# Last stage reordered into pairs of units, three banks for the up products and a ring of two for the rest; last states of the scan copied by ScalarE

## The reference, cut to what matters

```python
def _L1_attn_ref(...):          # x: 4096 tokens x 256, D_INNER = 512, N_STATE = 16
    ...
    def step(h, t):
        dt_t, B_t, C_t, u_t = t
        dA = jnp.exp(dt_t[:, :, None] * A)
        h = dA * h + (dt_t * u_t)[:, :, None] * B_t[:, None, :]
        return (h, jnp.einsum('bdn,bn->bd', h, C_t))
...
def _L1_ffn_ref(x, Wm, bm, expert_emb, W1, b1, W2, b2, Wo, bo):
    H, E, K = (8, 16, 2)         # heads of 32 features, experts, experts taken
    h = x @ Wm + bm
    t = h.reshape(bs * L_ * H, HD)
    w = jax.nn.softmax(t @ expert_emb, axis=-1)
    topw, topi = jax.lax.top_k(w, K)
    hmid = jax.nn.gelu(jnp.einsum('td,edi->tei', t, W1) + b1, approximate=False)
    eo = jnp.einsum('tei,eio->teo', hmid, W2) + b2
    sel = jnp.take_along_axis(eo, topi[:, :, None], axis=1)
    return (sel * topw[:, :, None]).sum(axis=1).reshape(bs, L_, d) @ Wo + bo
```

## Time and profile before

| | us |
|---|---|
| median of 3 runs | 3472.85 (3467.34 to 3473.31) |
| the profiled execution, its own time | 3465.27 |
| its span, first to last instruction | 3463.2 |
| first layer, up to about | 1665 |
| `layer1_scan`, about | 1665 to 2668 |
| `layer1_experts`: load and first routing | 2668 to 2722 |
| `layer1_experts`: 8 chunks | 2722 to 3441 |
| last projection, norm and store | 3441 to 3463 |

### The profile page before, as it was taken

One profiled execution on the slowest core, in us unless ns is written; L12 is line 12 of the kernel. 1 busy time (PEld: TensorE's weight loads), 2 busy tenths in 40 slices (PEclk: granted clock), 3 DMA queues, 4 the chain that ended last, 5 costly groups with the idle time before them and its releaser, 6 DMA issues. The chain is left out here.

```text
span 3463.2 us, 39510 instructions
## 1 busy us (share of the span) xinstructions
PE 3088.8 (89%) x11504; PEld 1701.8 (49%) x11504; DVE 2662.4 (77%) x3783; ACT 2282.6 (66%) x3239; POOL 2355.2 (68%) x1680
## 2 busy tenths in 40 slices
PE   3589999999999999998889999999976799999998
PEld 1156676666666667775334443443422333333332
DVE  5989898888988897554799999999996444544443
ACT  2457666666667666664666567666643488888887
POOL 3578888888888887773587888788783144444443
PEclk7689999999999999999899999999998799999999
DMA  2034444444444444553122222222221122222222
GB/s 94 13 97 128 122 128 126 127 121 119 131 123 121 124 120 130 146 148 87 61 68 70 71 69 69 71 70 68 71 70 55 53 99 99 105 105 104 103 101 86
DMA packets 199618, 335.38 MB, mean 97 GB/s; under 512 B 21379, under 2 KB 57380, under 8 KB 199020
## 3 DMA queue, kind: packets, MB, share of 16 engines
q1 hardware_dynamic: 199404, 332.86, 32.1%
HBM read 325.69 MB, written 7.09 MB: 96 GB/s over the span
## 5 line engine op out<-in xcount | busy, mean ns | idle before, releaser
L1435 POOL TENSOR_TENSOR c_hc<-c_h,c_c_rep 128x1024 f32<-128x1024 f32 x256 | 602.8, 2358 | 208.2 <-DVE c_h L1486 150.6
L1916 POOL TENSOR_TENSOR d_acc<-d_acc,d_prod 128x512 f32<-128x512 f32 x240 | 318.6, 1328 | 473.6 <-DVE d_prod L1984 473.2
L1486 DVE TENSOR_TENSOR_SCAN c_h<-c_decay,c_carry,c_v_ps 128x512 f32<-128x512 f32 x512 | 628.5, 1263 | 0.0
L1876 ACT ACTIVATE d_hmid<-d_up,d_b 128x1024 f32<-128x1024 f32 x512 | 539.7, 1112 | 78.4 <-PE d_up L1777 78.0
L1336 ACT ACTIVATE c_decay<-c_dt,c_a_cols 128x512 f32<-128x512 f32 x512 | 356.6, 718 | 337.0 <-DVE c_h L1486 319.9
L1186 PE MATMUL c_y_ps<-c_hc,ident 128*128 128x512 f32 x1024 | 507.1, 619 | 68.1 <-POOL c_hc L1435 56.1
L704 POOL TENSOR_TENSOR ab_inner_low<-ab_inner,ab_inner_high 128x512 fp32r<-128x512 f32 x264 | 341.1, 1292 | 239.5 <-ACT ab_inner_high L570 236.5
L559 ACT ACTIVATE ab_gate_ps<-ab_gate_ps,ab_raw_d 128x512 f32<-128x512 f32 x264 | 174.3, 660 | 445.7 <-PE ab_gate_ps L411 445.2
L1984 DVE SCALAR_TENSOR_TENSOR d_prod<-d_eo,d_b,d_w_rep 128x512 f32<-128x512 f32 x240 | 180.2, 751 | 314.9 <-PE d_eo L1787 172.8
L686 POOL TENSOR_TENSOR ab_hc<-ab_h,ab_c_rep 128x512 f32<-128x512 f32 x256 | 330.9, 1293 | 74.4 <-DVE ab_h L767 69.6
L1777 PE MATMUL d_up<-d_heads,d_w 128*128 128x512 f32 x1024 | 335.4, 434 | 16.6 <-ACT d_hmid L1876 9.4
(11 more groups left out here) (239 smaller groups left out, 6585.8 us busy)
## 6 DMA issues: line engine op xcount, KB each, us to landing
ab_raw_gu<-in_b_experts SPq DMA_DIRECT2D x264, 256.0 KB, 3.5
ab_w_rep<-ab_w_scratch SPq DMA_DIRECT2D x264, 256.0 KB, 3.7
c_c_rep<-c_c_scratch SPq DMA_DIRECT2D x256, 256.0 KB, 3.2
d_w_rep<-d_w_scratch SPq DMA_DIRECT2D x256, 256.0 KB
ab_raw_d<-in_b_experts SPq DMA_DIRECT2D x264, 129.0 KB, 2.1
ab_raw_x<-in_xT SPq DMA_DIRECT2D x32, 256.0 KB, 4.7
out<-xT SPq DMA_DIRECT2D x8, 512.0 KB, 3.4
xT<-in_xT SPq DMA_DIRECT2D x1, 3072.0 KB, 12.6
```

What stands on the lines that cost most here:

```text
L1435: nc.gpsimd.tensor_tensor(hc[:, q % HC], h[:, q % HR], c_rep[:, q % BC].unsqueeze(1).broadcast_to([P, PAIR, CH]), ALU.mult).then_inc(hc_re ...
L1486: nc.vector.tensor_tensor_scan(out=h[:, q % HR, m, :], data0=decay[:, i % DEC, :], data1=v_ps[m][:], initial=carry[:, i:i + 1], op0=ALU.mu ...
L1876: nc.scalar.activation(hmid[:, (2 * q + r) % HM], up_ps[r][:], ACT.Gelu, bias=b1[:, e:e + 1]).then_inc(gelu_ready, 1)
L1916: nc.gpsimd.tensor_tensor(acc[:, s, g, :], acc[:, s, g, :], prod[:, q % PR, :], ALU.add).then_inc(add_ready, 1)
```

## The change

**Scan.** `keep_last_states` moves from VectorE to ScalarE, as a copy of two columns per partition, behind the decays of unit `q`, for unit `q` - 4 (for q < 4 the last four units of the chunk before). The first scan of a unit now waits for that copy (`carry_ready`), as the copy must have read the slot of `h` that the scan overwrites.

**Experts, banks.** UP goes from 2 to 3 (six banks). The two banks left are a ring: all downs, the 13 items, the out projections, mean and variance take them in turn, in the order of the list `ring_uses`. Before a product, `take` waits for whoever reads the bank two uses before. HM goes from 4 to 8.

**Experts, order.** TensorE goes by pairs `u` of units: four `up` calls (eight products), then the two `down`s of the pair before, then items: halves at u = 0, 1; two heads each at u = 2..5; LOGITS at 6; TURN at 7; the variance of two chunks ago at 8 (before: of the last chunk, at q = 24); both out projections at 9, where the pair's last `up` comes behind them; mean at 10; BACK at 13. ScalarE and VectorE follow, two heads at a time.

```diff
@@ layer1_scan, scalar
+            def keep_last_states(c, q):
+                act.wait_ge(h_ready, c * NT + (q + 1) * PAIR + DEC)
+                nc.scalar.copy(carry[:, q * PAIR:(q + 1) * PAIR], h[:, q % HR, :, CH - 1]).then_inc(carry_ready, 1)
...
+                    if q >= HR:
+                        keep_last_states(c, q - HR)
+                    elif not first:
+                        keep_last_states(c - 1, NU - HR + q)
@@ layer1_scan, vector
-                    dve.wait_ge(carry_ready, c * NU + q + 1)
+                    dve.wait_ge(carry_ready, c * NU + q + 1 + NU - HR)
...
-            def keep_last_states(c, q):
-                dve.wait_ge(h_ready, c * NT + (q + 1) * PAIR + DEC)
-                nc.vector.reduce_max(carry[:, q * PAIR:(q + 1) * PAIR], h[:, q % HR, :, CH - 1:CH], axis=AX_X
-                                     ).then_inc(carry_ready, 1)
@@ layer1_experts
-    HM, UP, EO, PR, WR = 4, 2, 2, 4, 8
+    HM, UP, EO, PR, WR = 8, 3, 2, 4, 8
+    PAIRS = NU // 2
...
+    U_HALF, U_HEADS, U_LOGITS, U_TURN, U_VAR, U_OUT, U_MEAN, U_BACK = (0, 1), (2, 3, 4, 5), 6, 7, 8, 9, 10, 13
+    Q_SCALE, Q_EXP, Q_PICK, Q_SQUARE = 20, 17, 18, 23
+    def pair_uses(c, u):
+        if u > 0 or c > 0:
+            yield from (("down", c if u > 0 else c - 1, (2 * u - 2 + j) % NU) for j in range(2))
...
+        def bank(kind, c, i=0):
+            return ring[number[kind, c, i] % 2]
...
+            def take(kind, c, i=0):
+                at = number[kind, c, i]
+                if at >= 2:
+                    kind, c, i = ring_uses[at - 2]
+                    if kind == "down":
+                        pe.wait_ge(prod_ready, c * NU + i + 1 + EO)
+                    elif kind == "out":
+                        pe.wait_ge(norm.z_ready, c * 2 + i + 1 + norm.FREE)
+                    elif kind == "mean":
+                        pe.wait_ge(norm.zc_ready, c * 2 + 2)
+                    elif kind == "var":
+                        pe.wait_ge(norm.log_ready, c + 1)
...
@@ tensor, chunk
-                for q in range(NU):
+                for u in range(PAIRS):
                     for r in range(2):
-                        up(c, s, q, r)
-                    if q >= 1:
-                        down(c, q - 1)
-                    elif not first:
-                        down(c - 1, NU - 1)
...
+                        up(c, s, 2 * u, r)
+                    up(c, s, 2 * u + 1, 0)
+                    if u != U_OUT:
+                        up(c, s, 2 * u + 1, 1)
+                    for q in (2 * u - 2, 2 * u - 1):
+                        if q >= 0:
+                            down(c, q)
+                        elif not first:
+                            down(c - 1, NU + q)
                     if not last:
...
+                        if u in U_HEADS:
+                            product(c + 1, 1 - s, HEAD0 + 2 * (u - U_HEADS[0]))
+                            product(c + 1, 1 - s, HEAD0 + 2 * (u - U_HEADS[0]) + 1)
...
+                    if u == U_VAR and c >= 2:
+                        variance(c - 2)
+                    if u == U_OUT and not first:
+                        project_out(c - 1, 1 - s, 0)
+                        project_out(c - 1, 1 - s, 1)
+                    if u == U_MEAN and not first:
+                        mean(c - 1)
+                    if u == U_OUT:
+                        up(c, s, 2 * u + 1, 1)
```

More of the change, by code:

```diff
@@ L1605, in layer1_experts @@
     NADD = NU - GROUPS
-    HM, UP, EO, PR, WR = 4, 2, 2, 4, 8
+    HM, UP, EO, PR, WR = 8, 3, 2, 4, 8
+    PAIRS = NU // 2
     HEAD0, LOGITS, TURN, BACK = GROUPS, GROUPS + HEADS, GROUPS + HEADS + 1, GROUPS + HEADS + 2
     ITEMS = BACK + 1
-    Q_OUT, Q_MEAN, Q_CENTRE, Q_SQUARE, Q_VAR, Q_SCALE = 18, 20, 21, 23, 24, 20
-    Q_HALF, Q_HIGH, Q_LOW, Q_HEAD, Q_COPY = 0, 0, 1, 4, 5
-    Q_LOGITS, Q_KEEP_LOGITS, Q_TURN, Q_MAX, Q_EXP, Q_PICK, Q_BACK, Q_KEEP_WEIGHTS = 13, 13, 15, 16, 17, 18, 26, 26
+    U_HALF, U_HEADS, U_LOGITS, U_TURN, U_VAR, U_OUT, U_MEAN, U_BACK = (0, 1), (2, 3, 4, 5), 6, 7, 8, 9, 10, 13
[3 more added lines that the diff above has]
+            yield from (("down", c if u > 0 else c - 1, (2 * u - 2 + j) % NU) for j in range(2))
+        if c + 1 < NCH:
+            if u in U_HALF:
+                yield "item", c + 1, u - U_HALF[0]
+            if u in U_HEADS:
+                yield from (("item", c + 1, HEAD0 + 2 * (u - U_HEADS[0]) + j) for j in range(2))
+            for at, i in ((U_LOGITS, LOGITS), (U_TURN, TURN), (U_BACK, BACK)):
+                if u == at:
+                    yield "item", c + 1, i
+        if u == U_VAR and c >= 2:
+            yield "var", c - 2, 0
+        if u == U_OUT and c >= 1:
+            yield from (("out", c - 1, half) for half in range(2))
+        if u == U_MEAN and c >= 1:
+            yield "mean", c - 1, 0
+    ring_uses = [("item", 0, i) for i in range(ITEMS)]
+    for c in range(NCH):
+        for u in range(PAIRS):
+            ring_uses += pair_uses(c, u)
+    ring_uses += [("down", NCH - 1, NU - 2), ("down", NCH - 1, NU - 1), ("var", NCH - 2, 0)]
+    ring_uses += [("out", NCH - 1, 0), ("out", NCH - 1, 1), ("mean", NCH - 1, 0), ("var", NCH - 1, 0)]
+    number = {use: i for i, use in enumerate(ring_uses)}
+    assert len(number) == len(ring_uses)
     with ExitStack() as ctx:
@@ L1800, in project_out, with mean @@
                 for g in range(GROUPS):
-                    last = nc.tensor.matmul(work_ps[:], out_w[:, g, half * P:(half + 1) * P], acc[:, s, g, :],
+                    last = nc.tensor.matmul(bank("out", c, half)[:], out_w[:, g, half * P:(half + 1) * P], acc[:, s, g, :],
                                             start=(g == 0), stop=(g == GROUPS - 1))
                 last.then_inc(out_ready, 1)
+            def mean(c):
+                take("mean", c)
+                norm.mean(pe, c, bank("mean", c)[:])
@@ L1842, in _ @@
             over_chunks(pe, NCH, chunk)
+            down(NCH - 1, NU - 2)
             down(NCH - 1, NU - 1)
+            variance(NCH - 2)
             project_out(NCH - 1, 1, 0)
             project_out(NCH - 1, 1, 1)
-            norm.mean(pe, NCH - 1)
-            norm.variance(pe, NCH - 1)
+            mean(NCH - 1)
+            variance(NCH - 1)
         @block.scalar
@@ L1857, in keep_logits @@
                 act.wait_ge(work_ready, c * ITEMS + LOGITS + 1)
-                nc.scalar.copy(logit[:], work_ps[:]).then_inc(logit_kept, 1)
+                nc.scalar.copy(logit[:], bank("item", c, LOGITS)[:]).then_inc(logit_kept, 1)
             def exp(c):
@@ L1866, in keep_weights @@
                 act.wait_ge(w_stored, c * 16)
-                nc.scalar.copy(w_t[:], work_ps[:]).then_inc(wt_ready, 1)
+                nc.scalar.copy(w_t[:], bank("item", c, BACK)[:]).then_inc(wt_ready, 1)
             def chunk(c, s, first, last):
@@ L1883, in chunk @@
                         if not is_int(c, 0, 1):
-                            norm.deviation(act, c - 2)
+                            norm.deviation(act, c - 2, bank("var", c - 2)[:])
                         if not last:
@@ L1903, in _ @@
             over_chunks(act, NCH, chunk)
[L1904 removed]
+            norm.deviation(act, NCH - 2, bank("var", NCH - 2)[:])
             norm.square(act, NCH - 1)
[L1906 removed]
+            norm.deviation(act, NCH - 1, bank("var", NCH - 1)[:])
         @block.gpsimd
@@ L1983, in weigh @@
                     out = prod[:, q % PR, :]
-                nc.vector.scalar_tensor_tensor(out=out, in0=eo_ps[q % EO][:], scalar=b2[:, e:e + 1],
+                nc.vector.scalar_tensor_tensor(out=out, in0=bank("down", c, q)[:], scalar=b2[:, e:e + 1],
                                                in1=w_rep[:, q % WR, :], op0=ALU.add, op1=ALU.mult
@@ L2060, in _ @@
             residual(NCH - 1, 1)
-            norm.centre(dve, NCH - 1)
+            norm.centre(dve, NCH - 1, bank("mean", NCH - 1)[:])
             norm.scale(dve, NCH - 1)
```

164 lines of the change are left out of this document (78 added, 86 removed).

## The result

The changed kernel takes 3445.89 us (median of 8 runs, 3436.65 to 3450.48), the kernel before beside it 3468.18 (8 runs, 3458.19 to 3473.31): ratio 0.9936, 95% interval 0.992 to 0.9952, so 22 us faster. The forecast was 3450 with a range of 3430 to 3466, for a gain of 22.8. The profiled execution took 3446.60, 18.7 less than the one before.

The account below looks back on a forecast made before the run. Experts' stage bound by PE in pairs with two heads, ACT in pairs without items; scan by VectorE. Chunks -0.3, routing -9, scan -13.5 sum to -22.8: 3465.27 becomes 3442.5, or 3450 against the 3472.85 median; range 3430 to 3466.

Parts of the forecast that it names:

- The chain of a pair: Experts' stage, steps counted from a pair's first gelu to the next: pairs without items 4.39 us against 4.62.
- Heads, halves, pairs 8 to 10: Experts' stage, us per pair: two heads 5.93, halves 6.41 against 6.43, pair 8 10.35, pair 9 4.2, pair 10 6.3.
- the second rival: Experts' stage: the two banks make VectorE the bound, delayed weighs or copies costing 32 to 60 us, 3482; 8%, slower.
- Chunks 2 to 6: Experts' stage: +1.1 us a chunk, with +2.6 from pairs with two heads and -1.1 from pair 12; +5.5 for five.
- Chunk 1: Experts' stage: a stall of about 3 us on the spread weights goes, as a down comes a pair later: -2.8.
- Chunk 0: Experts' stage: heads cost +2.6 us, six pairs without items gain, no out, mean or deviation: +1.5.
- last chunk: Experts' stage: about 11 pairs without items at -0.23 us each, and pair 12: -3.5.
- The end: Tail: the two last out projections no longer share a bank, but scaling waits for the moved variance: -1 us.
- Routing before the first chunk: Two banks let five heads overlap, -5 us, and end VectorE's wait for the projection's second half, -4: -9, between -7 and -10.
- Scan: Reduction leaves VectorE, 16.5 us over 255 units, less 3 for waits on TensorE's spread of B: -13.5, bounds -9 and -17.
- the third rival: Scan gains nothing, as TensorE's records fill most of that stage too; the kernel ends near 3463.5 us; 12%.
- The first: Rival: the last stage becomes ScalarE's, then spread weights' loads hold a chunk at some 87 us, total 3425; 20%.

Follow-up runs that it names:

- late_fourth_up: The changed kernel with the fourth up of every pair behind the two downs: 3430.53 us, ratio 0.9893 to the kernel before.
- heads_before_downs: The changed kernel with a pair's two heads between its third and fourth up: 3433.90 us, ratio 0.9904 to the kernel before.
- experts_only: The changed kernel with the scan of before: 3458.91 us, ratio 0.9975 to the kernel before.
- scan_only: The kernel before with the scan's part of the change alone: 3453.42 us, ratio 0.9957 to it.
- store_by_scalar: The changed kernel with the store of the next chunk's weights issued by ScalarE, not SyncE: 3449.85 us, ratio 0.9955 to the kernel before.
- two_banks_first: The kernel before with only the 13 items before the first chunk going through two banks in turn: 3453.03 us, ratio 0.9962 to it.

## Why the prediction was right or wrong

- **The chain of a pair: right.** In a pair with heads every step came within 0.02 us. A plain pair takes 4.46 for 4.39: the downs' distance is at the lower bound (next product at G+3.68, not 3.73), but the gelu starts 0.77 behind its up, not 0.66. The 0.66 came from an up behind a head.
- **Heads, halves, pairs 8 to 10: right.** Heads 5.91, pair 8 10.43, pair 9 4.01, pair 10 6.32. `late_fourth_up` and `heads_before_downs` show the named waits as the cause.
- **Pair 12 gains 1.0 as forecast (5.48 to 4.46); pair 11 comes to 5.17.** VectorE's scaling and picks stand ahead of the centring there; it is where the second rival's mechanism was seen, and it decides little.
- **Chunks 2 to 6: +5.5, measured +7.0** (91.06 to 92.4 each). The size was off by 0.3 a chunk: pair 0 took 6.31 before and takes 6.43 (I had counted the halves as alike; 6.79 in chunk 6), and the plain pairs gained 0.15 each, not 0.23.
- **Chunk 1: -2.8, measured -0.2: wrong.** The step that failed was "since a down now comes a pair later, that stall goes". The stall hangs on when the store gets through the loads' queue: issued near the end of chunk 0, it landed 12.0 us later, where the median of the eight stores is 3.8, and pair 2 pays 1.7 us. Pair 3 pays 1.1 more, but at a granted clock of 0.76, and takes 5.92 in `experts_only`, whose last stage is the same, so that part is not the loads'. The size of the stall differs between profiles of one order, too: pair 2 took 8.51 before and 7.14 in `scan_only`, for 5.63 without a stall. `store_by_scalar` took both away (5.92, 5.91).
- **Chunk 0: +1.5, measured +0.1; last chunk: -3.5, measured -2.9.** Chunk 0 was already short of loads before: VectorE waited for one at every weighing of its pairs 2 to 5, which took 22.1 us instead of the 21.1 of later chunks, so the longer chain of the heads cost 1.5 there and not 2.6. It is 85 us both times.
- **The end: -1, measured +1.1.** The projections no longer share a bank, but two downs instead of one, and the variance, now stand behind the last gelus, and the last variance's products ran at a low clock. Since unchanged code gave 23.8 to 29.0 us there, the size can't be settled.
- **Routing before the first chunk: -9, measured -13.9.** What the forecast was made of came out: from the first product to the copy of the last head 31.1 us became 21.5, of which the halves gave 4.1 and the heads 5.4 (forecast 4 and 5); `two_banks_first` shows the same 21.4 with the banks alone. Of the rest, 2.3 lies ahead of the first product (1.8 of it in the scan stage's norm, whose products ran at a granted clock of 1.00 for 0.88) and 2.1 at LOGITS and TURN (1.00 for 0.50). The sum had no term for the clock. The 1.8 came with the shorter scan in every profile; the 2.1 followed neither half of the change: in the twelve kernels with two banks these products took 4.3 to 6.5 us.
- **Scan: -13.5, measured -11.7.** 0.06 for each of 255 units is 15.3, and 3.6 went back instead of 3. By the scans' starts six chunks gained 1.6 to 2.1 us, the first 0.4 (nine of its units are 3.67 long before and after) and the seventh 0.2. In the seventh VectorE now waits 1.4 us, in three places, for TensorE's spread of B, where it waited for nothing before; the longest of these waits falls in a stretch (2393.6 to 2398.0) with a granted clock of 0.71. `scan_only` shows the same 1.4. Part of this is the third rival's mechanism: TensorE fills the stage too.
- **The rivals.** The first (the last stage becomes ScalarE's and then meets the loads) did not happen, but its floor is real: it was put at 87 us a chunk, and `late_fourth_up` stands at 88. For it spoke the rule that changing the tiling mode drains TensorE (the Trainium skill, TensorEngine Tiling (Array Packing), Key Properties), priced at an estimated 25 us for half the changes. TensorE's records in the eight chunks fell by 27.3, which fits the rule without testing it, as the orders differ in more than that; the time is not there, as TensorE waited elsewhere. The slower one did not happen. The third did not either: the scan kept 11.7 of the 15.3.
- **The range.** The three spreads that the prediction names (-5 to +13, -1 to +2, -4 to +5) add up to 3440 to 3470, not to its 3438 to 3466; no other number hangs on that.

That the total was hit is partly luck: chunks and end missed by 5.5 us on one side, the routing by 4.9 on the other, the latter mostly by a clock that the sum had left out.

## What to carry to other kernels

On an engine that works in order, put what waits for nothing ahead of what waits, and fill each wait with work on another bank: nearly the same instructions in another order, with the store on another queue, brought 30 us beyond the 22 of the change. Before adding up such gains look for the floor behind them, here loads 2.60 us apart, and for what sets that floor, here the 32 packets one behind another in each stream and not the bytes. Price moves together, since two that each remove a wait may leave nothing to cover the next. Of a stall, ask which queue the late transfer stands in before expecting that later use will hide it.
